# Edge products in one 128-row fp32r pass over stacked high and low parts, in a graph network layer on one core

## The reference, cut to what matters

```python
N, C, E, ED, B, H = (8192, 256, 131072, 64, 256, 4)
ea = edge_attr @ w_e + b_e
msg = relu(x[src] + ea)
agg = segment_sum(msg, dst, num_segments=N)          # dst is sorted
t = x + agg
h_local = bn1(relu(t @ w1 + b1) @ w2 + b2 + x)
# attention inside blocks of 32 nodes, four heads
h_attn = bn2(attention(x) @ out_w.T + out_b + x)
out = h_local + h_attn
out = out + (relu(out @ m_w1 + m_b1) @ m_w2 + m_b2)
return layernorm(x + bn3(out))
```

## Time and profile before

| | us |
|---|---|
| median of 3 runs | 1351.08 |
| the profiled execution | 1350.94 |
| its span, first to last instruction | 1349.1 |
| PE busy | 1271.6 (94%) |
| PEld busy | 1022.4 (76%) |
| POOL busy | 984.5 (73%), in 1024 gathers |
| DVE busy | 904.6 (67%) |
| ACT busy | 751.4 (56%) |

### The profile page before, as it was taken

The page is one execution under the profiler, slowest core; times in us unless marked ns, Lnnn a source line. Parts: engine busy times, 40 slices in busy tenths (PEclk is TensorE's granted clock), DMA queues, the critical chain, the costliest instruction groups (busy, mean ns, idle before and its releaser), DMA issues.

```text
span 1349.1 us, 22612 instructions
## 1 busy us (share of the span) xinstructions
PE 1271.6 (94%) x8250; PEld 1022.4 (76%) x8250; DVE 904.6 (67%) x1763; ACT 751.4 (56%) x1617; POOL 984.5 (73%) x1032
## 2 busy tenths in 40 slices
PE   3778989999999999999999999999999999999997
PEld 2557777888878777787777787777777777787776
DVE  4998987666666666666666567666667666666662
ACT  1233334666666666566656556666566665665652
POOL 6777777777777777777777777777777777777740
PEclk6989999999999999999999999999999999999999
DMA  9777765555555555545555555555554555554531
GB/s 332 238 249 237 227 218 173 169 175 167 151 154 170 176 175 170 160 139 167 176 177 168 168 148 150 176 175 168 175 157 139 170 176 171 173 159 141 150 93 47
DMA packets 109648, 232.89 MB, mean 173 GB/s; under 512 B 21984, under 2 KB 46816, under 8 KB 109536
## 3 DMA queue, kind: packets, MB, share of 16 engines
q0 software_dynamic: 49152, 134.28, 34.6%
q1 hardware_dynamic: 58944, 93.87, 20.9%
q10 hardware_dynamic: 1440, 3.29, 0.7%
HBM read 206.19 MB, written 25.17 MB: 171 GB/s over the span
## 4 chain that ended last, share of the span: by engine, by line
POOL 39%; PE 23%; issue 14%; DMA 11%; DVE 6%; ACT 5%; SPq 0%; DVEq 0%; POOLq 0%; ACTq 0%
POOL xg L304 39%; DMA xg<-xb_dram,srcs 9%; PE both L677 6%; PE bank L707 5%; PE bank L677 5%; PE bank L722 5%; ACT bank L330 2%; ACT mh L334 1%; DMA aggT<-in_xT_dram 1%; DVE onehot L545 1%; DVE ml L533 1%; DVE bank L442 1%; DMA xrow<-in_x_dram 1%; PE bank L731 1%; DVE xrow L541 1%
## 5 line engine op out<-in xcount | busy, mean ns | idle before, releaser
L304 POOL DMA_INDIRECT xg<-xb_dram,srcs x864 | 817.8, 946 | 263.2 <-issue 228.2
L533 DVE SCALAR_TENSOR_TENSOR ml<-bank,mh 128x512 fp32r<-128x512 f32 x512 | 329.0, 684 | 240.4 <-ACT mh L334 239.0
L330 ACT COPY bank<-xg 128x512 f32<-128x512 f32 x432 | 256.2, 595 | 370.7 <-DMA xg<-xb_dram,srcs 353.8
L334 ACT ACTIVATE mh<-bank 128x512 fp32r<-128x512 f32 x512 | 276.3, 591 | 135.0 <-PE bank L707 134.4
L707 PE MATMUL bank<-we,ea 64*128 64x256 f32 x2048 | 296.6, 409 | 42.2 <-DVE bank L442 27.3
L707 PEld LDWEIGHTS bank<-we,ea 64*128 64x128 f32 x2048 | 180.4, 190 | 127.9 <-issue 73.9
L722 PE MATMUL bank<-mh,onehot 128*128 128x256 f32 x1024 | 263.9, 296 | 8.4 <-DVE onehot L545 8.4
L722 PE MATMUL bank<-ml,onehot 128*128 128x256 f32 x1024 | 250.7, 283 | 0.0
L722 PEld LDWEIGHTS bank<-mh,onehot 128*128 128x128 f32 x1024 | 195.2, 191 | 51.3 <-issue 38.3
L304 POOL DMA_INDIRECT xg<-in_x_dram,srcs x160 | 165.7, 1036 | 51.0 <-issue 47.2
L722 PEld LDWEIGHTS bank<-ml,onehot 128*128 128x128 f32 x1024 | 195.7, 191 | 0.0
(11 more groups left out here) (100 smaller groups left out, 1363.2 us busy)
## 6 DMA issues: line engine op xcount, KB each, us to landing
ea<-in_ea_dram SPq DMA_DIRECT2D x128, 256.0 KB
xg<-xb_dram,srcs POOLq DMA_INDIRECT x864, 3.3
xT<-in_xT_dram SPq DMA_DIRECT2D x32, 256.0 KB, 3.1
aggT<-in_xT_dram SPq DMA_DIRECT2D x32, 256.0 KB, 5.4
xrow<-in_x_dram SPq DMA_DIRECT2D x16, 512.0 KB, 5.8
xb_dram<-xrow SPq DMA_DIRECT2D x16, 512.0 KB, 2.7
oT_dram<-oT SPq DMA_DIRECT2D x32, 256.0 KB, 2.3
xn<-in_x_dram SPq DMA_DIRECT2D x32, 256.0 KB, 5.4
```

Source lines behind the costliest of these rows:

```text
L304: pool.indirect_dma_start(xg[:, q % NX, n * C:(n + 1) * C], None, t["x"] if q < XB_PAIR else k.xb_dram[:, :], bass.IndirectOffsetOnAxis(k. ...
L330: nc.scalar.copy(EA[q % 4][:, :], xg[:, q % NX, :]).then_inc(s_seed, 1)
L334: nc.scalar.activation(mh[:, q % NM, :], EA[q % 4][:, :], ACT.Relu).then_inc(s_mh, 1)
L533: nc.vector.scalar_tensor_tensor(ml[:, q % NM, :], EA[q % 4][:, :], 0.0, mh[:, q % NM, :].bitcast(fp32), ALU.max, ALU.subtract).then_inc(s ...
```

## The change

The attributes and the matrix w_e are split into a high part (rounded to fp32r) and a low part (the rest). `eahl` holds for each pair the 64 rows of one part above the 64 rows of the other, so that one matmul over 128 rows, in fp32r, adds both parts' products with a matrix that stands twice; `weh` and `wel` are its two parts. A 128 x 256 product is now two fp32r matmuls. The even and the odd pair no longer share the array.

Per group ScalarE rounds the 128 x 512 attributes into a free PSUM bank (`round_ea`) and writes the high part (`high_ea`, two 64 x 512 copies); VectorE subtracts the bank from the attributes (`low_ea`, two of 64 x 512). The free bank is `EA[a % 4]` of an odd turn, between `low` of its pair and the seed of the pair four later. ScalarE seeds all pairs by copies. For the pairs below 80, TensorE adds b_e with one more matmul per tile (a row of ones against b_e's two parts). `xb_dram` is made in 32 parts of 256 rows, one in every turn below 32. `ea` has two buffers, `xn` one; `ex` and `prob` take the place of `dif`, `we` and the gammas lie in buffers that are used later.

```diff
-NEA = 3
+NEA = 2
 AHEAD = 3
-XB = 16
+XB = 32
 XB_ROWS = N // XB // P
-XB_PAIR = XB * PG + 16
+XB_PAIR = 2 * XB + 16
...
-        k.we = sb("we", [P, C])
-        k.be_rows = sb("be_rows", [P, C])
+        k.weh, k.wel = sb("weh", [P, C], f32r), sb("wel", [P, C], f32r)
+        k.be_rows, k.be_hl = sb("be_rows", [P, C]), sb("be_hl", [P, C], f32r)
+        k.be_ones = sb("be_ones", [P, P], f32r)
...
+        k.ea, k.eahl = sb("ea", [P, NEA, 4 * P]), sb("eahl", [P, 2, 2, 4 * P], f32r)
...
+        k.ex = k.prob = k.dif
...
+        k.xn, k.y = sb("xn", [P, 1, 2, C]), sb("y", [P, 1, 2, C])
...
             def load_ea(n):
                 if n >= NEA:
-                    sp.wait_ge(s_prod, 2 * (n - NEA) + 2)
+                    sp.wait_ge(s_eah, n - NEA + 1)
+                    sp.wait_ge(s_eal, n - NEA + 1)
                 sp.dma_start(ea[:, n % NEA, :], t["ea"][n, :, :]).then_inc(s_ea[n % NEA], 16)
...
-                if turn % 2 == 1 and turn // 2 + 2 < NG:
-                    load_ea(turn // 2 + 2)
-                m = turn // 2
-                if turn % 2 == 1 and m < XB:
+                if turn == 0:
+                    load_ea(2)
+                if turn % 2 == 0 and turn // 2 + 3 < NG:
+                    load_ea(turn // 2 + 3)
+                m = turn
+                if m < XB:
                     sp.wait_ge(s_xadd, m + 1)
                     sp.dma_start(xb_parts[m, :, :, :], k.xrow[:, m % 2, :, :]
                                  ).then_inc(s_xbst[m % 2], 16)
-                if turn % 2 == 1 and 2 <= m + 1 < XB:
+                if 2 <= m + 1 < XB:
                     load_part(m + 1)
...
-                        if j >= 2:
-                            sp.wait_ge(s_r, j - 1)
-                        sp.dma_start(k.xn[:, j % 2, :, :], x_blocks[j, :, :, :]
+                        if j >= 1:
+                            sp.wait_ge(s_r, j)
+                        sp.dma_start(k.xn[:, 0, :, :], x_blocks[j, :, :, :]
...
-                if NX <= q < XB_PAIR + NX:
-                    pool.wait_ge(s_seedv, q - NX + 1)
-                if q >= XB_PAIR + NX:
-                    pool.wait_ge(s_seed, q - NX + 1 - XB_PAIR)
+                if q >= NX:
+                    pool.wait_ge(s_seed, q - NX + 1)
...
             def seed(q):
                 act.wait_ge(s_xg[q % NX], 32 * (q // NX + 1))
-                act.wait_ge(s_ml, q - 3)
+                if q < 4:
+                    act.wait_ge(s_set, 1)
+                else:
+                    act.wait_ge(s_ml, q - 3)
+                if q % 4 == 2 and 6 <= q and q // 4 + 2 <= NG:
+                    act.wait_ge(s_eal, q // 4 + 2)
                 nc.scalar.copy(EA[q % 4][:, :], xg[:, q % NX, :]).then_inc(s_seed, 1)
             def high(q):
                 act.wait_ge(s_prod, q // 2 + 1)
                 nc.scalar.activation(mh[:, q % NM, :], EA[q % 4][:, :], ACT.Relu
                                      ).then_inc(s_mh, 1)
+            def round_ea(n, bank):
+                act.wait_ge(s_ea[n % NEA], 16 * (n // NEA + 1))
+                nc.scalar.copy(bank[:, :].bitcast(f32r), ea[:, n % NEA, :]).then_inc(s_eab, 1)
+            def high_ea(n):
+                nc.scalar.copy(eahl[0:ED, n % 2, 0, :], ea[0:ED, n % NEA, :])
+                nc.scalar.copy(eahl[ED:P, n % 2, 1, :], ea[ED:P, n % NEA, :]).then_inc(s_eah, 1)
...
+            act.wait_ge(s_we, 16)
+            nc.scalar.copy(k.weh[:, :], k.we[:, :]).then_inc(s_weh, 1)
+            for n in range(2):
+                round_ea(n, X[1 + n])
+                high_ea(n)
+                if n == 0:
+                    seed(0)
+                    seed(1)
             for turn in range(TURNS):
                 a, b = 2 * turn, 2 * turn + 1
                 for q in (a + 2, b + 2):
-                    if XB_PAIR <= q < NP:
+                    if q < NP:
                         seed(q)
                 for q in (a, b):
                     if q < NP:
                         high(q)
+                n = (turn + 3) // 2
+                if turn % 2 == 1 and n < NG:
+                    act.wait_ge(s_ml, a + 1)
+                    round_ea(n, EA[a % 4])
                 if turn % 2 == 1 and 3 <= turn <= 2 * NG + 1:
                     copy_agg(turn // 2 - 1)
-                n = turn // 2 + 1
-                if turn % 2 == 0 and EA_PE <= n < NG:
-                    act.wait_ge(s_ea[n % NEA], 16 * (n // NEA + 1))
                 for i, step in heads_in(turn):
                     attention(i, step)
                 for j, step in nodes_in(turn):
                     node(j, step)
+                if turn % 2 == 0 and 2 <= turn // 2 + 1 < NG:
+                    high_ea(turn // 2 + 1)
...
-            def seed(q):
-                dve.wait_ge(s_xg[q % NX], 32 * (q // NX + 1))
-                if q < 4:
-                    dve.wait_ge(s_set, 1)
-                else:
-                    dve.wait_ge(s_ml, q - 3)
-                nc.vector.tensor_tensor(
-                    EA[q % 4][:, :].rearrange("p (t c) -> p t c", c=C),
-                    k.be_rows[:, :].unsqueeze(1).to_broadcast([P, 2, C]),
-                    xg[:, q % NX, :].rearrange("p (t c) -> p t c", c=C), ALU.add
-                ).then_inc(s_seedv, 1)
+            def low_ea(n, bank):
+                dve.wait_ge(s_eab, n + 1)
+                nc.vector.tensor_tensor(eahl[ED:P, n % 2, 0, :], ea[0:ED, n % NEA, :],
+                                        bank[0:ED, :], ALU.subtract)
+                nc.vector.tensor_tensor(eahl[0:ED, n % 2, 1, :], ea[ED:P, n % NEA, :],
+                                        bank[ED:P, :], ALU.subtract).then_inc(s_eal, 1)
...
             for turn in range(TURNS):
                 a, b = 2 * turn, 2 * turn + 1
-                for q in (a + 2, b + 2):
-                    if q < XB_PAIR:
-                        seed(q)
                 n = turn // 2
                 if turn % 2 == 0 and n >= 1:
                     if 2 <= n < NG + 2:
                         add_agg(n - 2)
-                    if n < XB:
-                        add_be(n)
                     if n < NG:
                         make_onehot(n)
+                if 1 <= turn < XB:
+                    add_be(turn)
                 for q in (a, b):
                     if q < NP:
                         low(q)
+                if turn % 2 == 1 and (turn + 3) // 2 < NG:
+                    low_ea((turn + 3) // 2, EA[a % 4])
...
             def products(d):
                 n, h = d // 2, d % 2
-                if h == 0 and n < EA_PE:
-                    pe.wait_ge(s_ea[n % NEA], 16 * (n // NEA + 1))
-                if 2 * d < XB_PAIR:
-                    pe.wait_ge(s_seedv, 2 * d + 2)
-                else:
-                    pe.wait_ge(s_seed, 2 * d + 2 - XB_PAIR)
-                for two in range(2):
-                    for pair in range(2):
-                        rows = slice(pair * ED, (pair + 1) * ED)
+                if h == 0 and n < 2:
+                    pe.wait_ge(s_eah, n + 1)
+                    pe.wait_ge(s_eal, n + 1)
+                pe.wait_ge(s_seed, 2 * d + 2)
+                for pair in range(2):
+                    for two in range(2):
                         at = (2 * h + two) * P
-                        ins = nc.tensor.matmul(EA[(2 * d + pair) % 4][:, two * C:(two + 1) * C],
-                                               ea[rows, n % NEA, at:at + P], k.we[rows, :],
-                                               start=False, stop=True,
-                                               skip_group_check=True)
+                        if 2 * d + pair < XB_PAIR:
+                            nc.tensor.matmul(EA[(2 * d + pair) % 4][:, two * C:(two + 1) * C],
+                                             k.be_ones[:, :], k.be_hl[:, :], start=False, stop=True,
+                                             skip_group_check=True)
+                        for half in (k.weh, k.wel):
+                            ins = nc.tensor.matmul(EA[(2 * d + pair) % 4][:, two * C:(two + 1) * C],
+                                                   eahl[:, n % 2, pair, at:at + P], half[:, :],
+                                                   start=False, stop=True, skip_group_check=True)
                 ins.then_inc(s_prod, 1)
```

More of the change, by code:

```diff
@@ L133, in program @@
     aggT, ident, vecT, s12 = k.aggT, k.ident, k.vecT, k.s12
-    xg, ea, mh, ml, onehot = k.xg, k.ea, k.mh, k.ml, k.onehot
+    xg, ea, eahl, mh, ml, onehot = k.xg, k.ea, k.eahl, k.mh, k.ml, k.onehot
     with ExitStack() as ctx:
@@ L150, in program @@
                                                          "s_c0_made", "s_m1_c0"))
-        s_bias = sem("s_biases_made")
+        s_bias, s_spread = sem("s_biases_made"), sem("s_base_copied")
         s_ea = [sem(f"s_edge_attr_{n}") for n in range(NEA)]
         s_xg = [sem(f"s_gathered_{n}") for n in range(NX)]
-        s_seedv = sem("s_x_b_e_seeded")
+        s_be = sem("s_be_split")
```

(26 more changed lines are left out.)

14 lines of the change are left out of this document (6 added, 8 removed).

## The result

The changed kernel takes 1382.61 us, the median of 4 runs (1378.75 to 1383.14); the kernel before beside it 1351.59 us (1350.74 to 1352.61). The ratio is 1.0219 with an interval of 1.0207 to 1.0231: 2.2% slower. The forecast was 1363. The sign, the place and the mechanism are as predicted, the size is not: 31 us instead of 12.

A forecast was written before the change was run, and what follows sets the result against it. POOL's gathers bound the kernel before; in the change fifteen opening loops of 12.4 us delay gather 149, then 1095.5 us of gathers to 1312.3 and the tail give span 1361.6, plus 1.84 outside: 1363.4 us. Range 1340 to 1386.

The forecast's parts named there:

- What bounds the kernel before: POOL's gathers, one per 1.2506 us, bound the span to 1299.5 us; then a TensorE tail of 49.6 us.
- The products: On TensorE, new products save 0.1 to 0.3 us per turn, worth nothing behind POOL except about 0.3 us in the tail.
- The seeds: 80 seeds leave VectorE, so 7.7 us of long gathers on POOL may go; 6.7 us at add_be stays.
- ScalarE and VectorE, steady: Their waits for each other take about 9.4 us per two turns against POOL's 10.0; nothing taken for it.
- rival B: ScalarE's and VectorE's waits for each other bound the kernel all along: 1390 to 1410 us; chance 0.08 together with another rival.
- The loop: In the opening, loading parts of x + b_e closes a two-turn loop of 8.4 us + L, 12.4 us; POOL needs 10.0.
- L: Landing of a part's 256 KB load in the opening, behind attributes and store: 4.0 us, between 2.7 and 5.5.
- The start of the loop: In the opening, the first part is added at 25 us and turn 2 ends on ScalarE at 35 us.
- After gather 149 and the tail: POOL can't catch up: 1095.5 us of gathers up to 1312.3, then a tail of 49.6 - 0.3 us.
- The rule that was weighed: Skill's DMA fit, 2.0 us plus bytes at 436 GB/s, gives L = 2.8 and 1345 us; not followed.
- Rival A: Loads of parts come in time and POOL stays the bound from its first gather: 1343, down to 1337 us; chance 0.32.

The follow-up runs named there:

- experiment 6: Kernel before with SyncE's load of part m + 1 ahead of the store of part m, nothing else: 1351.16 us, ratio 0.9993.
- experiment 7: Kernel before with add_be cut to one column, so b_e is missing from nearly all of x + b_e: 1344.65 us, ratio 0.9925.
- version 2: Changed kernel with SyncE's order of each turn load, store, attributes: 1343.44 us, run again 1340.22 us, ratio 0.9926 to the kernel before both times.
- experiment 9: Every matmul of the groups' sums issued twice, in the kernel before and in the changed kernel with load, store, attributes order: 1551.24 and 1500.71 us.
- experiment 3: Changed kernel with SyncE's load ahead of the store, load_ea still in front of both: 1362.79 us, ratio 1.0073 to the kernel before.
- experiment 4: Changed kernel with the attributes of groups 3 to 18 loaded in 8 columns of 512 only: 1369.2 us, ratio 1.0124 to the kernel before.
- experiment 5: Kernel before with x + b_e in 32 parts of 256 rows, add_be, store and load in every turn: 1361.33 us, ratio 1.0065.
- experiment 1: Changed kernel with load_ea moved behind the store and the load on SyncE's queue: 1359.3 us, ratio 1.0041 to the kernel before.

## Why the prediction was right in sign and wrong in size

*What bounds the kernel before: right.* Where POOL's gathers change, the time follows by about as much: nothing in experiment 6, 10 us (7 to 13) in 7 for 8.3 us of shorter gathers, 10 us (8 to 12) in version 2 for 10.4. (The trace has 41 gathers over 1.0 us after the first in these 160, not 43.)

*The products: right.* 0.1 to 0.3 us per turn were forecast, 0.23 measured (experiment 9), behind POOL and so worth nothing. In the middle of the changed kernel a turn's eight products start 0.20 us (the first) and seven times 0.12 us apart, 1.03 us until the sum's first matmul, which follows at the same pace, with no 0.23 us as in the earlier trace rows:

```profile
704.56 0.36 PE L751 MATMUL bank<-weh,eahl 128*128 128x256 f32 x1
704.76 0.28 PE L751 MATMUL bank<-wel,eahl 128*128 128x256 f32 x1
...
705.59 0.28 PE L765 MATMUL bank<-mh,onehot 128*128 128x256 f32 x1
```

*The seeds: right.* The 7.7 us of long gathers at seeds are gone once POOL is the bound again; and of the 6.7 us at `add_be` a part went too (10.4 us in all in version 2), which I had left out.

*ScalarE and VectorE, steady: right.* 80 or 81 gathers per 100 us from 300 us on; rival B falls. (Its price has a slip: 0.1 us in 112 pairs of turns is 11 us and not 1.1; its 45 for 0.4 is right.) POOL waits for a seed at 258.10 and 264.21 us, 1.5 us beyond its usual 0.30; I had said that it would not wait after 217 us. One or two such waits near the last pairs with b_e on TensorE are in experiments 2 and 3 too; their cause is open.

*The loop: right in every step but one.* The rest of it was forecast at 8.4 us and is 8.29. **The step that failed is the size of L, the landing of a 256 KB load behind the attributes and a store: 4.0 us taken, 5.03 measured.** Fifteen times 1.03 us are 15.5; the rest of the loop, 0.1 shorter, gives 1.6 back. I had taken more than a third off 5.8 us for half the bytes and put back a few tenths for the attributes. Experiments 3 and 4 show what was too low: the store in front is worth 1.07 us of L and the attributes' bytes 0.88, and with one of the two away it is near 4.0 (3.96 and 4.15). It lay inside my bounds (2.7 to 5.5), so the range held the time. But eight turns took four loops, 53.3 us, where I had said 46 to 52 if I was right.

Why a transfer in front costs what it does stays open; their number alone doesn't tell. Behind a store alone, loads of the same size land after 3.64 us in the odd turns of the changed kernel (mean of fifteen, 2.72 to 5.40), 4.43 on the chain of experiment 5 and 4.77 on that of experiment 1.

*The start of the loop: 2.3 us off.* Turn 2 was to end on ScalarE at 35 us; SyncE issues the attributes behind it at 37.28 (the first part is added at 26.79 us and not at 25, and a seed waits 1.53 us for `low_ea` on the way):

```profile
26.79 0.69 DVE L581 TENSOR_TENSOR xrow<-be_rows,xrow 128x512 f32<-128x512 f32 x1 [10.03 <-DMA xrow<-in_x_dram]
...
34.01 1.11 ACT L343 COPY bank<-xg 128x512 f32<-128x512 f32 x2 [1.53 <-DVE eahl L473]
...
37.28 0.33 SPq L209 DMA_DIRECT2D ea<-in_ea_dram  x1
```

With these two sizes the sum reads 37.3 + 15 x 13.3 = 236.8, less 4.2: 232.6, and the trace has 232.75. That it fits so well is in part luck: in the first of the fifteen rounds (37.28 to 51.43 us) the chain runs through TensorE, not through the load, and takes 14.15 us.

*After gather 149 and the tail.* From its start to the last one's end I had 1095.5 us; it is 1098.3. The tail is 50.4 and not 49.3. Together 3.9 us. 16.0 + 3.9 bring the forecast span of 1361.6 to 1381.5, where the trace has 1381.4.

*The rule that was weighed.* The Trainium skill, DMA: Bandwidth & Descriptors, section Anatomy of one DMA, has a fit of 2.0 us plus the bytes at 436 GB/s, for the GpSimd path. An estimate by it is 3.8 us for the 768 KB, so 2.8 from the load's own issue, 1 us after that of the attributes. The trace does not agree: 4.96 us, and no landing of the eleven is under 3.97. The measurement decides.

*Rival A* (the loads come in time) didn't come about in the change, since its condition, a loop under 10.3 us, wasn't met. Its price was about right: 1343 forecast for it, 1343.4 and 1340.2 measured in experiment 2, both 0.9926 of the kernel before (10 us less, where the forecast had 8), where another order on SyncE's queue brings the loads in time.

## What to carry to other kernels

When a wait on a queue of transfers is moved to a later event, ask what stands behind it on that queue: here a load that needed neither the attributes nor the store was held by both, and that alone turned a change worth 0.7% into one that costs 2.2%. Put on the queue first what is ready first. And when a buffer is cut in half, the round trip through it is not: its fixed part, with `add_be` and the issues, then has to fit in half the time.

## What the runs showed of the hardware that I had not expected

- How long a 256 KB load takes to land depends on what was issued just ahead of it on its queue: 3.16 us in the mean with nothing directly in front (odd turns of experiment 3), 3.96 behind 256 KB of attributes (even turns there), 5.03 behind the attributes and a 256 KB store. Behind a store alone the means are 3.64, 4.43 and 4.77 us in three of the kernels, so there is no fixed amount for a transfer.
- 8 columns instead of 512 in the attributes' load (4 KB instead of 256 KB) shorten the landing of the load two places behind it by 0.88 us.
- Gathers on POOL get longer beside VectorE's additions of two operands in SBUF, up to 2.00 us for one of 0.95 us. I had seen it in the trace, but not expected how much it is worth: 0.75% of the whole time (0.5 to 1.0%) for `add_be` alone (experiment 7).
